# First stage of a fused four-layer kernel: x loaded a second time, already turned, and block loads shared by two queues

## The chip, the cores and the metric

The kernel runs on one NeuronCore of a Trainium2 chip. The metric is the device time of one execution in microseconds (us), as the median of several runs. Below, PE is TensorE, PEld its weight loads, ACT is ScalarE, DVE is VectorE, POOL is GpSimd and SP is SyncE; SPq and ACTq are the instructions with which SyncE and ScalarE issue transfers.

## What is computed

x has 32 batches of 64 channels of 1024 values (f32). Four layers follow one another, each as x = x + ffn(cond(x)). Only the first one is touched:

```
cond, layer 0: out[b] = agg_w[b] (64x64) @ x[b] + agg_b[b]
ffn, layer 0:  logits = out @ route_w^T (8 experts); best one e, its logit v
               h = out @ A^T (8 experts x 16); keep the 16 of e, times v
               ffn = kept h @ Bw
x = x + ffn                      (called x1 below)
cond, layer 1: grouped convolution of x1 along the 1024 values, 9 taps
```

Layers 1 to 3 are a quantised matmul with a row maximum, a routed LoRA layer, and a two-matrix feed-forward with a latent branch and a layer norm.

## The kernel before, in words

The work is cut into NT = 16 tiles of 128 rows (two batches of 64 channels), each 128 x 1024 values, 512 KB. `build` runs `phase_setup`, then `phase_l0` (the first stage), each a block of its own that ends with a barrier of all engines, and then one block for the other three layers, which begins with the convolved tiles of the first stage and with their column maxima. The changed stage, `phase_l0`, contains layer 0 and the convolution of layer 1, as a pipeline over steps s.

In step s TensorE does, in this order: `ph(s)`, the product of the turned tile s with the 136 columns of A and the router (L587); the first half of the convolution of tile s-4 (L437, L438); `mix(s)`, the mixing of the 64 channels (L596); the second half of that convolution; the turning of tile s+1, eight transposes into two PSUM banks (L607); `po(s-1)`, the product with Bw (L614); and the turning of the gated 128 x 128 block of tile s (L619). ScalarE does the copy of ph into h_in (L503), the shifted copies Xs of tile s-3 (L451, L452), for which it waits until all eight block loads of that tile have landed, the two copies of the turned tile s+1 from PSUM into xT (L515), and the copy of the turned gated block, whT (L520). mix(s+1) waits for whT(s) and for h_in(s+1). VectorE finds the best expert (L537 to L552), adds ctx to the convolution result into y1T (L527), takes the column maximum (L559) and adds po to the tile in place, which makes x1 (L566).

SyncE issues all transfers of the stage, tile after tile: it waits for x1 of tile t, stores it to a scratch tensor (L488), waits until the store has landed, loads x of tile t+4 into the slot that came free (L491), and then issues eight block loads of 64 KB each (L446, in `load_windows`) that read the stored tile back as X, the 1024 values cut into eight blocks spread over the partitions:

```
view = dram.rearrange("t (n c) (p k) -> t p c n k", n=2 * GROUPS, p=KC)
for p in range(KC):
    sp.dma_start(dst[p * GI:(p + 1) * GI, :, :], view[t, p]).then_inc(sem, 16)
```

Each block load writes 16 partitions in runs of 512 bytes. The x tiles sit in four slots, X and Xs in three. In `phase_setup` SyncE loads the first four tiles of x (L253); the buffer y1T, 16 slots of one tile, holds weights in its slots 0 to 13 during setup and is filled with the convolved tiles 0 to 15 later. `load_windows` is also called in the block of the later layers (L740); there SyncE issues in each round the store of y2T (L696), in eight rounds a load of 512 KB (L749), the store of x2 (L734, `scratch_x<-l_x`), and waits for that store before the block loads. `eps` is one f32 per partition, used as the bias of a square root in the last layer (L1562); the larger SBUF buffers but for y1T and l2_base are allocated behind it.

Of the kernel before, what the change touches and what calls it, by code (L numbers as in the profile page):

```python
# [11 lines left out]
P = 128  # L12
# [167 lines left out]
def phase_setup(nc, K, A, SC):  # L180


    with ExitStack() as ctx:
# [42 lines left out]
        def _(sp):  # L226
# [25 lines left out]
            for t in range(4):  # L252
                sp.dma_start(K["x"][:, t, :], A["x"][t]).then_inc(K["x_loaded"][t], 16)  # L253
            sp.wait_ge(bias3_out, 1)
# [187 lines left out]
def load_windows(sp, dram, t, dst, sem):  # L442

    view = dram.rearrange("t (n c) (p k) -> t p c n k", n=2 * GROUPS, p=KC)
    for p in range(KC):
        sp.dma_start(dst[p * GI:(p + 1) * GI, :, :], view[t, p]).then_inc(sem, 16)  # L446
# [8 lines left out]
def phase_l0(nc, K, A, SC):  # L455
# [3 lines left out]
    with ExitStack() as ctx:  # L459
        s_ = Scope(nc, ctx)  # L460
        wa, wb, x, X, Xs = K["l0_wa"], K["l0_wb"], K["x"], K["X"], K["Xs"]
        xT = s_.sb("xT", [P, KC, P])
# [7 lines left out]
        pt = s_.banks("pt", 2)  # L470
# [5 lines left out]
        (xT_mm, xT_made, h_mm, hp_made, m_mm, route, wh_made, wh_turned, whT_made, o_mm, x1_made, Xs_made, conv_done,  # L476
         y_made, topped) = s_.sems(
            "xT_mm xT_made h_mm hp_made m_mm route_step wh_made wh_turned whT_made o_mm x1_made Xs_made conv_done "
# [5 lines left out]
        @block.sync  # L484
        def _(sp):
            for t in range(NT):
                sp.wait_ge(x1_made, 2 * (t + 1))
                sp.dma_start(SC["x1"][t], x[:, t % 4, :]).then_inc(x1_stored[t % 4], 16)  # L488
                sp.wait_ge(x1_stored[t % 4], 16 * (t // 4 + 1))
                if t + 4 < NT:  # L490
                    sp.dma_start(x[:, t % 4, :], A["x"][t + 4]).then_inc(K["x_loaded"][t % 4], 16)  # L491
                if t >= 3:
                    sp.wait_ge(conv_done, 2 * (t - 2))
                load_windows(sp, SC["x1"], t, X[t % 3], X_loaded[t % 3])

        @block.scalar
        def _(act):
            for s in range(-1, NT + LAG - 1):
                if 0 <= s < NT:
                    act.wait_ge(h_mm, s + 1)  # L500
                    if s >= 1:
                        act.wait_ge(m_mm, s)
                    act.copy(hp[:], ph[:, 0:P + E0]).then_inc(hp_made, 1)  # L503
                t = s - 3
                if 0 <= t < NT:
                    act.wait_ge(X_loaded[t % 3], 16 * KC * (t // 3 + 1))
                    if t >= 3:
                        act.wait_ge(conv_done, 2 * (t - 2))
                    shift_windows(act, Xs[t % 3], X[t % 3], Xs_made)
                if s + 1 < NT:  # L510
                    for i in range(2):
                        act.wait_ge(xT_mm, 2 * (s + 1) + i + 1)
                        if s >= 0:
                            act.wait_ge(h_mm, s + 1)
                        act.copy(xT[:, 4 * i:4 * i + 4, :], pt[i][:].rearrange("k (p o) -> k p o", p=4)).then_inc(xT_made, 1)  # L515
                if 0 <= s < NT:
                    act.wait_ge(wh_turned, s + 1)
                    if s >= 1:
                        act.wait_ge(o_mm, 2 * s)
                    act.copy(whT[:], pm[:, 2 * P:3 * P]).then_inc(whT_made, 1)  # L520

        @block.vector
        def _(dve):
# [6 lines left out]
            for s in range(NT + LAG):  # L530
# [30 lines left out]
                if 0 <= s - 1 < NT:  # L561
                    slot = x[:, (s - 1) % 4, :]
                    for i in range(2):
                        dve.wait_ge(o_mm, 2 * (s - 1) + i + 1)
                        half = slice(i * HALF, (i + 1) * HALF)
                        dve.tensor_tensor(slot[:, half], po[i][:], slot[:, half], ALU.add).then_inc(x1_made, 1)  # L566
# [3 lines left out]
        def _(pe):  # L570
# [10 lines left out]
            for s in range(-1, NT + LAG):  # L581
                if 0 <= s < NT:
                    pe.wait_ge(xT_made, 2 * (s + 1))
                    if s >= 1:
                        pe.wait_ge(hp_made, s)
                    for k in range(KC):
                        last = pe.matmul(ph[:, 0:P + E0], xT[:, k, :], wa[:, k, :], start=k == 0, stop=k == KC - 1)  # L587
# [11 lines left out]
                if s + 1 < NT:  # L599
                    t = s + 1  # L600
                    pe.wait_ge(K["x_loaded"][t % 4], 16 * (t // 4 + 1))
                    for i in range(2):
                        if t >= 1:
                            pe.wait_ge(xT_made, 2 * (t - 1) + i + 1)
                        for j in range(4):
                            k = 4 * i + j
                            last = pe.transpose(pt[i][:, j * P:(j + 1) * P], x[:, t % 4, k * P:(k + 1) * P], K["ident"][:])  # L607
                        last.then_inc(xT_mm, 1)
# [63 lines left out]
def phase_l1(nc, K, A, SC, s_, buf, ahead):  # L672
# [55 lines left out]
    def sync(sp):  # L728
# [7 lines left out]
        def windows_in(t):  # L736
# [3 lines left out]
            load_windows(sp, SC["x2"], t, X[t % 3], X_loaded[t % 3])  # L740
# [673 lines left out]
def phase_l3(nc, K, A, SC, out, s_, buf):  # L1414
# [122 lines left out]
    def scalar(act):  # L1537
# [15 lines left out]
        def norm(half):  # L1553

            for T in range(HT * half, HT * (half + 1)):
# [6 lines left out]
                act.activation(root[:, T:T + 1], ssq[:, T:T + 1], ACT.Sqrt, bias=eps[:], scale=1.0 / D).then_inc(rooted, 1)  # L1562
# [237 lines left out]
def build(nc, A, out):  # L1800
# [8 lines left out]
    with ExitStack() as ctx:  # L1809
# [10 lines left out]
        K["x_loaded"] = s.slot_sems("x_loaded", 4)  # L1820
# [3 lines left out]
        K["eps"] = s.sb("eps", [P, 1])  # L1824
# [65 lines left out]
def lay_out(i):  # L1890
# [16 lines left out]
    a["x"] = c(feat(i["x"])).reshape(NT, P, D)  # L1907
    cut = {"cT": np.asarray(i["cond_128"]).T}
# [58 lines left out]
```

## Time and profile before

| | |
|---|---|
| median of 3 runs | 1857.82 us (1857.61 to 1861.25) |
| the profiled execution's own time | 1855.62 us |
| its span | 1853.8 us |
| mean granted TensorE clock | 0.973 |
| TensorE busy | 1741.4 us (94%) |
| bytes moved by DMA | 205.80 MB |

The profiled execution stands 2.2 us below the median. A busy time is a sum over the instructions of an engine; idle time of an engine costs something only where the others wait for it. In the timelines each row gives start, duration, engine, line and what is written from what; a bracket at the end tells how long the engine had been idle and who released it. In a timeline of TensorE an f32 product stands as two matmuls. In this text T(t) is the moment at which the store of x1 of tile t has landed, and mix(s) stands for the start of that matmul.

### The profile page before, as it was taken

What the parts mean: (1) busy time and instruction counts of PE and PEld (TensorE: products, weight loads), DVE (VectorE), ACT (ScalarE), POOL (GpSimd) and SP (SyncE); (2) the same over time, 40 slices, a digit from 0 to 9 for tenths busy, and PEclk for the clock granted to TensorE, in tenths of its full rate; (3) what the DMA queues carried; (4) which work ended last, traced back from release to release, by engine and by line L of the source; (5) the groups of instructions that cost most, each with busy time, mean ns of one, the idle gap of its engine ahead of it and who ended that gap; (6) DMA issues with size and microseconds to landing.
All of it is one profiled execution on the core that took longest, in us unless ns stands there. A gap on an engine that the chain in (4) does not pass through costs nothing.

```text
span 1853.8 us, 22240 instructions
## 1 busy us (share of the span) xinstructions
PE 1741.4 (94%) x8396; PEld 1412.5 (76%) x8396; DVE 824.0 (44%) x1453; ACT 459.5 (25%) x694; POOL 340.2 (18%) x186
## 2 busy tenths in 40 slices
PE   7899847999799999999999999999999999999997
PEld 3578736878678888888668888888777888888876
DVE  4256578985524433443323333333272333333326
ACT  2344323433311111111132222221123222222212
POOL 1000011234223333333311111111201111111110
PEclk9899978999899999999999999999999999999999
DMA  8377323566533223332751111111292111111114
GB/s 308 95 193 191 114 71 124 180 194 220 207 97 117 93 95 106 117 93 83 200 178 56 46 46 45 45 45 46 98 333 69 46 46 46 45 45 45 46 57 159
DMA packets 126803, 205.80 MB, mean 111 GB/s; under 512 B 14436, under 2 KB 82092, under 8 KB 126124
## 3 DMA queue, kind: packets, MB, share of 16 engines
q1 hardware_dynamic: 109716, 158.41, 26.8%
q0 software_dynamic: 11264, 27.27, 4.6%
q10 hardware_dynamic: 5760, 19.27, 3.2%
q8 instruction: 42, 0.69, 0.2%
q14 instruction: 21, 0.17, 0.0%
HBM read 143.01 MB, written 61.89 MB: 111 GB/s over the span
## 4 chain that ended last, share of the span: by engine, by line
PE 72%; DVE 6%; DMA 5%; SPq 1%; issue 1%; ACT 1%; POOL 0%; DVEq 0%; ACTq 0%
PE pd L1410 24%; PE pu L1410 24%; PE l_po L1410 18%; PE pf L1410 2%; DMA scratch_x<-l_x 2%; PE l_py L1384 1%; PE l_pr L1368 1%; DVE row_peak L836 1%; DMA l_base_lo<-scratch_y_lo 1%; SPq L446 1%; DMA l_B_raw<-in_l_B 1%; DMA scratch_y_lo<-y_out_lo 1%; PE l_pc L1334 1%; DVE y1T L861 1%; ACT row_mag L791 1%
## 5 line engine op out<-in xcount | busy, mean ns | idle before, releaser
L1410 PE MATMUL pu<-l_base_hi,up_hi 128*128 128x512 f32 x640 | 253.4, 396 | 0.0
L1410 PE MATMUL pu<-l_base_lo,up_hi 128*128 128x512 f32 x640 | 252.9, 395 | 0.0
L1410 PE MATMUL pu<-l_base_hi,up_lo 128*128 128x512 f32 x640 | 252.9, 395 | 0.0
L1410 PE MATMUL pd<-down_hi,hid_hi 128*128 128x512 f32 x640 | 250.1, 391 | 2.9 <-issue 2.9
L1410 PE MATMUL pd<-down_hi,hid_lo 128*128 128x512 f32 x640 | 249.5, 390 | 0.0
L1410 PE MATMUL pd<-down_lo,hid_hi 128*128 128x512 f32 x640 | 249.5, 390 | 0.0
L1533 POOL TENSOR_TENSOR down_lo<-raw,down_hi 128x1024 fp32r<-128x1024 f32 x40 | 100.4, 2511 | 716.4 <-ACT down_hi L1546 716.4
L1698 DVE TENSOR_TENSOR hid_lo<-hidden,hid_hi 128x512 fp32r<-128x512 f32 x64 | 44.8, 701 | 406.4 <-ACT hid_hi L1607 406.4
L1638 DVE TENSOR_TENSOR acc<-pd,acc 128x512 f32<-128x512 f32 x224 | 144.0, 686 | 56.4 <-PE pd L1410 53.5
L1601 ACT ACTIVATE hidden<-pu 128x512 f32<-128x512 f32 x64 | 38.3, 598 | 474.5 <-PE pu L1410 474.5
L1410 PEld LDWEIGHTS pd<-down_hi,hid_hi 128*128 128x128 f32 x640 | 120.1, 188 | 29.7 <-issue 3.7
L1410 PEld LDWEIGHTS pu<-l_base_hi,up_lo 128*128 128x128 f32 x640 | 120.1, 188 | 29.4
L1410 PEld LDWEIGHTS pu<-l_base_hi,up_hi 128*128 128x128 f32 x640 | 120.1, 188 | 28.9
L1410 PEld LDWEIGHTS pu<-l_base_lo,up_hi 128*128 128x128 f32 x640 | 120.1, 188 | 28.7
L1410 PEld LDWEIGHTS pd<-down_hi,hid_lo 128*128 128x128 f32 x640 | 120.1, 188 | 26.0
L1410 PEld LDWEIGHTS pd<-down_lo,hid_hi 128*128 128x128 f32 x640 | 120.1, 188 | 25.9
L1410 PE MATMUL pf<-cbT,z_hi 128*128 128x512 f32 x256 | 108.1, 422 | 18.3 <-DVE z_lo L876 18.1
L1410 PE MATMUL l_po<-l_B_hi,crT_hi 128*128 128x512 f32 x256 | 103.2, 403 | 3.5 <-DVE crT_lo L1255 3.5
L1264 DVE TENSOR_TENSOR l_y<-l_py,l_bias 128x512 f32<-128x512 f32 x32 | 22.1, 692 | 187.0 <-issue 97.0
L1410 PE MATMUL pf<-cbT,z_lo 128*128 128x512 f32 x256 | 104.7, 409 | 0.0
L1410 PE MATMUL l_po<-l_base_hi,l_y2s_hi 128*128 128x512 f32 x256 | 103.9, 406 | 0.0
L1410 PE MATMUL l_po<-l_base_hi,l_y2s_lo 128*128 128x512 f32 x256 | 101.2, 395 | 0.0
(244 smaller groups left out, 2850.9 us busy)
## 6 DMA issues: line engine op xcount, KB each, us to landing
X<-scratch_x SPq DMA_DIRECT2D x256, 64.0 KB, 2.7
l_x<-scratch_x SPq DMA_DIRECT2D x32, 512.0 KB, 4.8
raw<-in_up SPq DMA_DIRECT2D x32, 512.0 KB, 3.5
raw<-in_down SPq DMA_DIRECT2D x32, 512.0 KB, 4.2
x_in<-in_x SPq DMA_DIRECT2D x16, 512.0 KB, 4.2
scratch_x<-x_in SPq DMA_DIRECT2D x16, 512.0 KB, 3.3
scratch_x<-l_x SPq DMA_DIRECT2D x16, 512.0 KB, 5.1
scratch_y2T<-y2T SPq DMA_DIRECT2D x16, 512.0 KB, 3.0
```

The costliest lines, as they stand in the source:

```text
L446: sp.dma_start(dst[p * GI:(p + 1) * GI, :, :], view[t, p]).then_inc(sem, 16)
L791: act.activation(mag[:, 0:n, p, :], y[:, t0:t0 + n, 4 * i + p, :], ACT.Abs, scale=keep[:, 4 * i + p:4 * i + p + 1]).then_inc(mag_made, 1)
L836: dve.tensor_reduce(peak[:, i, 0:n, :].unsqueeze(3), mag[:, 0:n, :, :].rearrange("k t p j -> k t j p"), AX.X, ALU.max).then_inc(peaked, 1)
L861: dve.tensor_tensor(y[:, t0 + j, :, :], y[:, t0 + j, :, :], pb[:, j * P:(j + 1) * P].unsqueeze(1).to_broadcast([P, KC, P]), ALU.mult).then ...
L1264: dve.tensor_tensor(y3[:, h * HALF:(h + 1) * HALF].rearrange("p (c k) -> p c k", c=4), py[h][:].rearrange("p (c k) -> p c k", c=4), bias3[ ...
L1334: last = pe.transpose(pc[h][:, j * P:(j + 1) * P], cr[:, k * P:(k + 1) * P], K["ident"][:])
L1368: last = pe.matmul(pr[0][0:R2 + E2, 0:P], war[:, k, :], y2[:, k * P:(k + 1) * P], start=k == 0, stop=k == KC - 1)
L1410: mm = pe.matmul(out, lhs[a], rhs[b], start=first and n == 0, stop=last and n == len(pairs) - 1)
L1533: pool.tensor_tensor(dn[u][i][1][:], raw[i][:], dn[u][i][0][:].bitcast(F32), ALU.subtract).then_inc(dn_lo, 1)
L1601: act.activation(act_f[:, k % 2, :], pu[q], ACT.Relu).then_inc(relu, 1)
L1638: last = dve.tensor_tensor(part, bank, part, ALU.add)
L1698: dve.tensor_tensor(hid[u][1][:, i, cols], pu[q] if lat else act_f[:, k % 2, :], hid[u][0][:, i, cols].bitcast(F32), ALU.subtract).then_in ...
```

## The change

- x is also laid out turned on the host (`xT`: tile, value within a block, block, row), 16 more tiles of 512 KB in. The slots for it are the slots 14, 15, 12 and 13 of y1T. Tiles 0 and 1 are loaded in setup between the x tiles, tiles 2 and 3 at the start of the stage, and tile t+4 by SyncE in its iteration t, ahead of the store of x1(t), once ph(t) is done.
- TensorE's eight transposes of a tile and ScalarE's two copies are gone. ph(s) waits for the load of its turned tile.
- SyncE issues five of the eight block loads of a tile in the first stage, ScalarE the other three, in step s for tile s-2, behind its copies Xs of tile s-3 and ahead of whT(s). For that it waits for the landed store of tile s-2. In the later layers SyncE issues all eight, as before.
- VectorE waits for the load of the x tile, to which it adds.
- eps has 16 values per partition instead of one; the first is used.

```diff
@@ phase_setup, SyncE
             for t in range(4):
                 sp.dma_start(K["x"][:, t, :], A["x"][t]).then_inc(K["x_loaded"][t], 16)
+                if t < 2:
+                    sp.dma_start(K["xT"][t], A["xT"][t]).then_inc(K["xT_loaded"][t], 16)
@@
-def load_windows(sp, dram, t, dst, sem):
+def load_windows(eng, dram, t, dst, sem, phases):
...
-    for p in range(KC):
-        sp.dma_start(dst[p * GI:(p + 1) * GI, :, :], view[t, p]).then_inc(sem, 16)
+    for p in phases:
+        eng.dma_start(dst[p * GI:(p + 1) * GI, :, :], view[t, p]).then_inc(sem, 16)
@@ phase_l0, SyncE
+            for t in range(2, 4):
+                sp.dma_start(K["xT"][t], A["xT"][t]).then_inc(K["xT_loaded"][t], 16)
             for t in range(NT):
+                if t + 4 < NT:
+                    sp.wait_ge(h_mm, t + 1)
+                    sp.dma_start(K["xT"][t % 4], A["xT"][t + 4]).then_inc(K["xT_loaded"][t % 4], 16)
                 sp.wait_ge(x1_made, 2 * (t + 1))
...
-                load_windows(sp, SC["x1"], t, X[t % 3], X_loaded[t % 3])
+                load_windows(sp, SC["x1"], t, X[t % 3], X_loaded[t % 3], range(5))
@@ phase_l0, ScalarE
-                if s + 1 < NT:
-                    for i in range(2):
-                        act.wait_ge(xT_mm, 2 * (s + 1) + i + 1)
-                        if s >= 0:
-                            act.wait_ge(h_mm, s + 1)
-                        act.copy(xT[:, 4 * i:4 * i + 4, :], pt[i][:].rearrange("k (p o) -> k p o", p=4)).then_inc(xT_made, 1)
-                if 0 <= s < NT:
+                t = s - 2
+                if 0 <= t < NT:
+                    act.wait_ge(x1_stored[t % 4], 16 * (t // 4 + 1))
+                    if t >= 3:
+                        act.wait_ge(conv_done, 2 * (t - 2))
+                    load_windows(act, SC["x1"], t, X[t % 3], X_loaded[t % 3], range(5, KC))
+                if s < NT:
                     act.wait_ge(wh_turned, s + 1)
@@ phase_l0, VectorE
                     slot = x[:, (s - 1) % 4, :]
+                    dve.wait_ge(K["x_loaded"][(s - 1) % 4], 16 * ((s - 1) // 4 + 1))
@@ phase_l0, TensorE
-                    pe.wait_ge(xT_made, 2 * (s + 1))
+                    pe.wait_ge(K["xT_loaded"][s % 4], 16 * (s // 4 + 1))
...
-                        last = pe.matmul(ph[:, 0:P + E0], xT[:, k, :], wa[:, k, :], start=k == 0, stop=k == KC - 1)
+                        last = pe.matmul(ph[:, 0:P + E0], K["xT"][s % 4][:, k, :], wa[:, k, :], start=k == 0, stop=k == KC - 1)
...
-                if s + 1 < NT:
-                    t = s + 1
-                    pe.wait_ge(K["x_loaded"][t % 4], 16 * (t // 4 + 1))
-                    for i in range(2):
-                        if t >= 1:
-                            pe.wait_ge(xT_made, 2 * (t - 1) + i + 1)
-                        for j in range(4):
-                            k = 4 * i + j
-                            last = pe.transpose(pt[i][:, j * P:(j + 1) * P], x[:, t % 4, k * P:(k + 1) * P], K["ident"][:])
-                        last.then_inc(xT_mm, 1)
@@ build
+        K["xT"] = [K["y1T"][:, t, :, :] for t in (14, 15, 12, 13)]
-        K["eps"] = s.sb("eps", [P, 1])
+        K["eps"] = s.sb("eps", [P, 16])
@@ lay_out
+    a["xT"] = c(a["x"].reshape(NT, P, KC, P).transpose(0, 3, 2, 1))
```

## Rows read from the trace of the kernel before

**Rows 1.** The page: busy us of each engine, share of the span, instructions.

```profile
PE 1741.4 (94%) x8396; PEld 1412.5 (76%) x8396; DVE 824.0 (44%) x1453; ACT 459.5 (25%) x694; POOL 340.2 (18%) x186
```

**Rows 2.** Stretches: busy us of PE, PEld, DVE, ACT, POOL; clock, DMA share, GB/s.

```profile
75.00:84.00 9.00, 7.63 (x32) 6.94 (x33) 0.74 (x3) 1.44 (x3) 0.00 (x0) 0.50 0.01 3
...
104.90:108.00 3.10, 3.08 (x14) 3.08 (x15) 0.00 (x0) 0.14 (x1) 0.00 (x0) 0.52 1.06 205
108.00:202.00 94.00, 94.00 (x714) 82.91 (x713) 57.16 (x121) 42.05 (x69) 0.00 (x0) 1.00 0.67 186
```

**Rows 3.** Timeline of TensorE, one step in the middle (convolutions left out).

```profile
148.25 2.02 PE L587 MATMUL ph<-l_wa,xT 128*128 128x136 f32 x16
...
151.89 0.40 PE L596 MATMUL pmix<-h_in,mats 128*128 128x136 f32 x2
...
153.91 1.04 PE L607 MATMUL pt<-ident,x_in 128*128 128x128 f32 x8
154.78 1.88 PE L614 MATMUL po<-l_wb,whT 128*128 128x512 f32 x4
...
156.61 1.56 PE L587 MATMUL ph<-l_wa,xT 128*128 128x136 f32 x12
```

**Rows 4.** Timeline of SyncE's transfers, first tiles; last row: what L491 waited for.

```profile
91.49 0.33 SPq L488 DMA_DIRECT2D scratch_x<-x_in  x1
94.12 0.33 SPq L491 DMA_DIRECT2D x_in<-in_x  x1
94.50 3.74 SPq L446 DMA_DIRECT2D X<-scratch_x  x8
98.28 0.43 SPq L488 DMA_DIRECT2D scratch_x<-x_in  x1
102.61 0.35 SPq L491 DMA_DIRECT2D x_in<-in_x  x1
...
110.89 0.35 SPq L491 DMA_DIRECT2D x_in<-in_x  x1
...
SPq L491 <- DMA scratch_x<-x_in: 36.6, 12, 3.9
```

**Rows 5.** Timeline of TensorE, start and end of the stage.

```profile
75.33 1.94 PE L607 MATMUL pt<-ident,x_in 128*128 128x128 f32 x8 [4.68 <-PEq L104]
77.95 3.99 PE L587 MATMUL ph<-l_wa,xT 128*128 128x136 f32 x16 [0.68 <-ACT xT L515]
...
104.92 3.55 PE L587 MATMUL ph<-l_wa,xT 128*128 128x136 f32 x16 [3.24 <-ACT xT L515]
...
202.05 0.40 PE L596 MATMUL pmix<-h_in,mats 128*128 128x136 f32 x2
```

**Rows 6.** ScalarE: the first wait for block loads; the copies of the turned tile.

```profile
101.67 1.04 ACT L451 COPY Xs<-X 64x1016 f32<-64x1016 f32 x1 [3.25 <-DMA X<-scratch_x]
...
L515 ACT COPY xT<-pt 128x512 f32<-128x512 f32 x32 | 17.3, 589 | 17.7 <-PE pt L607 17.7
```

**Rows 7.** The chain of waits in the second layer: start us, us, what.

```profile
402.81 0.36 SPq L696
403.22 0.43 SPq L749
403.69 5.91 DMA scratch_x<-l_x
...
414.64 7.20 DMA scratch_x<-l_x
...
426.50 6.63 DMA scratch_x<-l_x
```

**Rows 8.** ScalarE's own transfers in the third layer: ns of one issue.

```profile
L1195 ACTq DMA_DIRECT2D l_y<-scratch_y2T x14: 344/344/372, 510.1 to 851.7; - x14
```

**Rows 9.** VectorE groups: one on buffers allocated before eps, one behind it.

```profile
L410 DVE TENSOR_REDUCE w_scb<-y1T 128x1 f32<-128x1024 f32 x8 | 9.4, 1214 | 10.0 <-DMA y1T<-in_L_ffn_weight 9.9
...
L1245 DVE TENSOR_TENSOR l_B_lo<-l_B_raw,l_B_hi 128x1024 fp32r<-128x1024 f32 x8 | 9.2, 1221 | 9.6 <-ACT l_B_hi L1189 9.6
```

More of the change, by code:

```diff
@@ L469, in phase_l0 @@
         key, gain = small[:, 8:16], small[:, 16:24]
-        pt = s_.banks("pt", 2)
         (ph,) = s_.banks("ph", 1)
@@ L475, in phase_l0 @@
         x1_stored, X_loaded = s_.slot_sems("x1_stored", 4), s_.slot_sems("X_loaded", 3)
-        (xT_mm, xT_made, h_mm, hp_made, m_mm, route, wh_made, wh_turned, whT_made, o_mm, x1_made, Xs_made, conv_done,
+        (h_mm, hp_made, m_mm, route, wh_made, wh_turned, whT_made, o_mm, x1_made, Xs_made, conv_done,
          y_made, topped) = s_.sems(
-            "xT_mm xT_made h_mm hp_made m_mm route_step wh_made wh_turned whT_made o_mm x1_made Xs_made conv_done "
+            "h_mm hp_made m_mm route_step wh_made wh_turned whT_made o_mm x1_made Xs_made conv_done "
             "y1_made y1_topped")
@@ L493, in _ @@
                     sp.wait_ge(conv_done, 2 * (t - 2))
-                load_windows(sp, SC["x1"], t, X[t % 3], X_loaded[t % 3])
+                load_windows(sp, SC["x1"], t, X[t % 3], X_loaded[t % 3], range(5))
         @block.scalar
         def _(act):
-            for s in range(-1, NT + LAG - 1):
-                if 0 <= s < NT:
+            for s in range(NT + LAG - 1):
+                if s < NT:
                     act.wait_ge(h_mm, s + 1)
@@ L509, in _ @@
                     shift_windows(act, Xs[t % 3], X[t % 3], Xs_made)
-                if s + 1 < NT:
-                    for i in range(2):
-                        act.wait_ge(xT_mm, 2 * (s + 1) + i + 1)
-                        if s >= 0:
-                            act.wait_ge(h_mm, s + 1)
-                        act.copy(xT[:, 4 * i:4 * i + 4, :], pt[i][:].rearrange("k (p o) -> k p o", p=4)).then_inc(xT_made, 1)
-                if 0 <= s < NT:
+                t = s - 2
[4 more added lines that the diff above has]
+                    load_windows(act, SC["x1"], t, X[t % 3], X_loaded[t % 3], range(5, KC))
+                if s < NT:
                     act.wait_ge(wh_turned, s + 1)
@@ L579, in conv @@
                 conv_windows(pe, pv[b][:], K["taps"][0], X[t % 3], Xs[t % 3], b).then_inc(conv_done, 1)
-            for s in range(-1, NT + LAG):
-                if 0 <= s < NT:
-                    pe.wait_ge(xT_made, 2 * (s + 1))
+            for s in range(NT + LAG):
+                if s < NT:
+                    pe.wait_ge(K["xT_loaded"][s % 4], 16 * (s // 4 + 1))
                     if s >= 1:
@@ L739, in windows_in @@
                 sp.wait_ge(conv_done, 2 * (t - 2))
-            load_windows(sp, SC["x2"], t, X[t % 3], X_loaded[t % 3])
+            load_windows(sp, SC["x2"], t, X[t % 3], X_loaded[t % 3], range(KC))
         for s in range(NT):
@@ L1561, in norm @@
                 act.wait_ge(ssq_made, T + 1)
-                act.activation(root[:, T:T + 1], ssq[:, T:T + 1], ACT.Sqrt, bias=eps[:], scale=1.0 / D).then_inc(rooted, 1)
+                act.activation(root[:, T:T + 1], ssq[:, T:T + 1], ACT.Sqrt, bias=eps[:, 0:1], scale=1.0 / D).then_inc(rooted, 1)
                 if 0 < T % HT < HT - 1:
@@ L1819, in build @@
         K["x3b_loaded"], K["y3_loaded"] = s.slot_sems("x3b_loaded"), s.slot_sems("y3_loaded")
-        K["x_loaded"] = s.slot_sems("x_loaded", 4)
+        K["x_loaded"], K["xT_loaded"] = s.slot_sems("x_loaded", 4), s.slot_sems("xT_loaded", 4)
+        K["xT"] = [K["y1T"][:, t, :, :] for t in (14, 15, 12, 13)]
         K["g_stored"] = s.slot_sems("g_stored")
```

1 line of the change is left out of this document (removed).

## The prediction

> **What bounds the kernel now.** The page first: TensorE is busy in 94% of the span [rows 1], so idle time elsewhere says little by itself. The changed stage lies between two barriers, about 75 to 232 us; what is saved in it moves the rest forward as a block, and nothing behind the second barrier can hide it. So only the stage has to be read, and I cut it into stretches [rows 2]. From 108 to 202 TensorE is busy without a gap at full clock while the DMA engines are busy 0.67 of the time. The timeline of one step shows why [rows 3]: ph starts at 148.25 and the next ph at 156.61, a period of 8.36 us, in which the eight transposes take 0.87 (153.91 to 154.78). In the middle of the stage TensorE ends last.
>
> The second reading is SyncE's queue [rows 4], because it runs nearly as long. At the start, where TensorE's steps hold no convolution and are short, SyncE sets the pace: load of x at 94.12, again at 102.61 and 110.89, cycles of 8.49 and 8.28, mean 8.4. Such a cycle is one load issue, eight block loads (3.74, so 0.47 each), one store issue, and 4.3 (98.28 to 102.61) until that store has landed. A store with nothing ahead of it lands in 2.6 (91.49 to 94.12). Over the stage the wait before L491 is 36.6 us in 12 [rows 4], 3.05 each; with the store's 0.34 and the rest of the cycle (0.38 + 3.74 + 0.04) it needs 7.6 without any queueing behind its own backlog and 8.4 with it. So SyncE stands only 0 to 0.8 behind TensorE's 8.36, and whoever shortens TensorE's step meets SyncE at once.
>
> **The change, part by part.**
>
> *Transposes gone.* 0.87 per step where TensorE binds: 8.36 - 0.87 = 7.49 is TensorE's new period. Over the 11 steps from mix(4) to mix(15) that is at most 9.6 us.
>
> *Copies gone.* ScalarE loses 32 x 0.589 = 17.3 us [rows 6]. Twice these copies were on the path. At the start, ph(0) waited for transposes and copies: 75.33 to 77.95, 2.6 us [rows 5]; this goes, the turned tile 0 is loaded in setup. At step 4 ph stood 3.24 us behind them, because ScalarE was held at 101.67 by the first block loads, and then ran 104.92 to 108.47 at a clock of 0.52 [rows 2, 5, 6], the lower level of 1.2 GHz, after the idle stretch. What is late next there is the shifted copy itself, which still waits for the block loads.
>
> *Loads of xT.* 16 issues. Tiles 0 and 1 queue in setup, where SyncE has nothing to issue for some 20 us before the barrier; tiles 2 and 3 are issued while SyncE would wait for its first store at 91.49. Priced at nothing; if that cover failed, a queue of two transfers would delay setup by 1.2 each, 2.4. From tile 4 on each stands in SyncE's queue ahead of the store: 0.47 for the issue, and the store queues behind its data. The nearest rows are in the second layer [rows 7]: two transfers of this size (L696, L749) stand between the block loads and the store there, and the store takes 5.91, 7.20 and 6.63 to land, mean 6.6, against 4.3 right behind the block loads: 1.15 for each transfer, at most 1.45. Bounds: 0, if the data fit into the third of the time in which the DMA engines are idle [rows 2], and 1.45. I take 1.2, as rows 7 have the same queue and size.
>
> *Three block loads to ScalarE.* SyncE issues 3 x 0.47 = 1.41 less per cycle. ScalarE pays 3 x 0.344 [rows 8] plus gaps, 1.2, behind a wait for the landed store. Queued behind them are whT(s) and h_in(s+1), for both of which mix(s+1) waits. So mix(t+3) starts no sooner than T(t) + 1.2 + 0.3 + 0.3, about T(t) + 2.0. In the steady step mix starts 3.6 after ph (148.25, 151.89), so this wait has that room and costs nothing unless SyncE is late.
> The row says that SyncE's issue time is on the cycle: its store at 98.28 goes out as soon as the last block load is issued (98.24). The Trainium skill (DMA: Bandwidth & Descriptors, section Issuing engines are not separate DMA queues) speaks against this part: transfers issued by several engines run on the same 16 DMA engines, and only the issue time is saved, usually small beside the transfer. By that rule read strictly, with the data as the bound, the 1.41 would not come off; what this would give is the third rival.
>
> *SyncE's new cycle c.* 8.4 + 0.47 + 1.2 - 1.41 = 8.66 from the cycles in which it sets the pace. The same from the cycle without backlog, 7.6, is 7.9. I take 8.5, nearer the first, since SyncE would now always set the pace.
>
> *eps and the wait on x.* Where buffers begin changes for nearly everything. A reduction that reads y1T (before eps) takes 1214 ns, a subtraction with all operands behind it 1221 [rows 9]: the place makes no visible difference. Bounds -1 to +1 us, taken 0. VectorE's wait is for a load issued some three steps earlier: 0.
>
> **The sum.** ph(0) starts 2.6 earlier, so the first store would go out at 91.49 - 2.6 = 88.9; I add 0.6: until 84 the granted clock is 0.50 [rows 2], a ph at it takes 3.99 [rows 5] against 2.02 [rows 3], and with the transposes gone TensorE does less there, so the rise may come later; 0.6 is a third of that difference. With 2.6 to land, T(0) = 92.1. SyncE then needs twelve cycles to T(12), the last without a turned tile (1.6 less): 92.1 + 12 x 8.5 - 1.6 = 192.5. mix(15) follows at +2.0: 194.5, against 202.05 [rows 5], so 7.5 saved. At the end of the stage the chain is store, block loads, shifted copy, convolution; SyncE issues three block loads less before the last store and three less behind it, 1.41 twice at most, of which I take 1.6, since x1 of the last tile is not ready much earlier. Together 9.1. Against the profiled execution's own 1855.62 this gives 1846.5; the median lies 2.2 above it, so **1848.7**.
>
> **The rivals.**
>
> *TensorE stays the bound* (c at most 7.5). For it: the DMA engines are busy only 0.67 of the time [rows 2], and the lower estimate of c, 7.9, is not far off. Against it: the landings in rows 7. mix(4) would come at T(1) + 2.0 to 2.3 = 101.9, mix(15) 11 x 7.49 later at 184.3, 17.8 earlier, with the end 19.4: 1838.4.
>
> *The queue gives half back* (c about 9.2). xT's data cost their full 1.45 and half of the 1.41 returns as queueing. T(12) = 92.1 + 110.4 - 1.6 = 200.9, mix(15) 202.9, 0.8 late, the end 1.6 early: 1857.0, no change that can be told.
>
> *Slower: transfers bind.* Before, a cycle moved three tiles' worth (x, block loads, store); now four, on the same DMA engines, with a share of 1.06 at only 205 GB/s in 104.9 to 108 [rows 2], where block loads and a store meet. If the data are the bound, the 1.41 saved in issuing come back whole: c = 8.5 + 1.41 = 9.9, T(12) = 209.3, mix(15) 211.3, 9.2 late, less 1.6: 7.6 slower, 1865.4. It decides from c = 9.26 on (92.1 + 12c - 1.6 + 2.0 = 203.65). Against it: 4 tiles in 9.9 us would be only 212 GB/s. This is also where the Trainium skill leads (same page and section as above); the trace bears it out in part, since in the middle the share is far from 1.
>
> *The change does less than it says*: that xT makes ph wait. It is issued three steps ahead, so only if the whole queue is late, which is the rival before. 0.03, time near before.
>
> **How the numbers follow.** About 0.2% (3.7 us) is what a measurement of this kernel can tell from no change. c from 8.0 to 8.9 (15.1 to 4.3 saved): 0.48. c under 8.0 or TensorE the bound: 0.20. c from 8.9 to 9.6 (4.3 saved to 4.1 lost) 0.17, with the change that does less 0.03. c above 9.6: 0.12. Faster is the first two and a little of the third, 0.70; within 0.2% 0.18; slower 0.12. The range reaches from TensorE as the bound, 1838, to c = 9.3 and a lost microsecond in setup, 1859; it leaves out about 0.05 below and 0.14 above.
>
> **What would show it.** L607 and L515 gone; first ph near 75.3; 8.4 MB more moved. The cycle of L491 in the middle at 8.5 with the store landing in 5 to 5.5, and small gaps on TensorE before mix, released by ScalarE. If instead TensorE is gapless with period 7.5, the first rival holds; if the share of the DMA engines is near 1 and the store takes 7, the third. ScalarE's three issues far over 0.4 each would be a wait that I have not priced. Matmuls of the later layers longer or shorter than before would prove me wrong on eps.

## The result, and the profile after

The changed kernel takes 1867.34 us (median of 10 runs, 1864.68 to 1870.30) against 1855.93 (median of 10, 1849.22 to 1861.25) for the kernel before on the same chip: ratio 1.0063, 95% interval 1.0050 to 1.0075. It is slower, by some 11 us. The forecast was 1848.7 with a range up to 1859. The profiled execution took 1870.0, its span is 1868.2 and the mean granted clock 0.974, as before.

The page first, busy time of each engine as in [rows 1]:

```profile
PE 1725.1 (92%) x8268; PEld 1400.4 (75%) x8268; DVE 824.2 (44%) x1453; ACT 441.0 (24%) x662; POOL 340.1 (18%) x186
```

TensorE has 128 instructions and 16.3 us less, ScalarE 32 instructions and 18.5 us less, and the time went up: work was taken away and waiting came in. Where it came in is told by the first instruction behind the second barrier, VectorE's column maximum; here it is in the timeline of VectorE, before and then after.

```profile
232.23 0.38 DVE L890 TENSOR_REDUCE col_max<-col_top 128x8 f32<-128x128 f32 x1 [1.25 <-PEq L104]
```

```profile
250.35 0.38 DVE L886 TENSOR_REDUCE col_max<-col_top 128x8 f32<-128x128 f32 x1 [1.22 <-PEq L104]
```

The changed stage ends 18.1 us later. What follows takes 1868.2 - 250.35 = 1617.9 against 1853.8 - 232.23 = 1621.6, so 3.7 us less. These are two separate effects.

Stretches of the kernel after, with the columns of [rows 2]:

```profile
75.00:84.00 9.00, 6.08 (x24) 5.48 (x25) 1.49 (x6) 0.54 (x2) 0.00 (x0) 0.50 0.49 176
...
108.00:202.00 94.00, 75.88 (x500) 63.27 (x499) 48.24 (x101) 22.60 (x36) 0.00 (x0) 0.96 0.81 204
```

In the middle of the stage TensorE was busy for 94.00 of 94 us before; now it is busy for 75.88. Over the whole stage, by the same view from 75 us to its end, it works 6.7 us less (137.28 against 143.99) and idles 24.8 us more (38.0 against 13.2): together the 18.1. The DMA engines' share in the middle rose from 0.67 to 0.81.

SyncE's queue, in the timeline of its transfers, is the view that explains it (compare [rows 4]):

```profile
91.22 0.33 SPq L493 DMA_DIRECT2D scratch_x<-x_in  x1
93.84 0.33 SPq L496 DMA_DIRECT2D x_in<-in_x  x1
...
97.06 0.43 SPq L493 DMA_DIRECT2D scratch_x<-x_in  x1
...
145.29 0.33 SPq L496 DMA_DIRECT2D x_in<-in_x  x1
145.67 2.33 SPq L448 DMA_DIRECT2D X<-scratch_x  x5
148.04 0.43 SPq L491 DMA_DIRECT2D y1T<-in_xT  x1
148.52 0.43 SPq L493 DMA_DIRECT2D scratch_x<-x_in  x1
155.41 0.33 SPq L496 DMA_DIRECT2D x_in<-in_x  x1
...
209.65 0.43 SPq L493 DMA_DIRECT2D scratch_x<-x_in  x1
215.35 2.20 SPq L448 DMA_DIRECT2D X<-scratch_x  x5
```

The first store still lands in 2.62 (91.22 to 93.84). In the middle the issue of x load, five block loads, turned load and store takes 3.66 us (145.29 to 148.95), less than before, but the store takes 6.89 to land (148.52 to 155.41), and nothing else happens in SyncE meanwhile. The cycle is 155.41 - 145.29 = 10.12. The waits of SyncE in this stage say the same:

```profile
SPq L496 <- DMA scratch_x<-x_in: 74.7, 12, 7.6
...
SPq L493 <- DVE x_in L572: 11.1, 1, 11.1
```

The wait for the landed store before the load of x was 36.6 in 12 [rows 4] and is 74.7 in 12. The last line matters as much: only once, for the first tile, does the store wait for x1. From then on SyncE is held by its own chain alone: store landed, x load, block loads, turned load, store.

How the data run inside one such cycle, in stretches with the same columns:

```profile
145.30:147.30 2.00, 2.00 (x15) 2.00 (x16) 0.00 (x0) 0.44 (x2) 0.00 (x0) 0.81 0.24 67
147.30:148.50 1.20, 1.20 (x8) 1.20 (x7) 0.69 (x2) 0.00 (x0) 0.00 (x0) 0.50 0.96 367
148.50:150.50 2.00, 2.00 (x14) 2.00 (x13) 1.39 (x6) 0.00 (x0) 0.00 (x0) 0.64 1.25 187
150.50:152.50 2.00, 2.00 (x9) 0.99 (x8) 1.54 (x2) 0.00 (x0) 0.00 (x0) 1.00 1.16 194
152.50:155.40 2.90, 2.13 (x19) 1.96 (x17) 1.56 (x3) 2.08 (x2) 0.00 (x0) 1.00 0.66 263
```

What moves there is told by the size of the packets, in the view of the DMA queues for the third of these stretches (the runs of a block load are 512 bytes; these 792 packets hold 470 bytes on average):

```profile
DMA packets 792, 0.37 MB, mean 187 GB/s; under 512 B 91, under 2 KB 788, under 8 KB 792
```

First almost nothing moves (67 GB/s, the transfers are only being issued), then mostly the x load, at 367 GB/s. Then for 2 us nearly all packets are those of block loads, at 187 GB/s and a share of the DMA engines of 1.25, and for 2 us more the last of them (233 of 303 packets) together with the turned load, at 194. Only then the rest of the turned load and the store follow. The turned load lands at 154.1, 6.1 us after its issue, and the store 1.3 us behind it. The mean of 0.81 hides that the engines are full just while the store waits in line.

On the other engines: ph(0) at last starts at once, but it and the next ph run at the lower clock (1.2 GHz, granted 0.50), and TensorE has no gap before mix(4). TensorE's timeline:

```profile
75.80 3.96 PE L593 MATMUL ph<-l_wa,y1T 128*128 128x136 f32 x16 [4.68 <-PEq L104]
...
82.97 3.83 PE L593 MATMUL ph<-l_wa,y1T 128*128 128x136 f32 x16
...
105.42 0.50 PE L602 MATMUL pmix<-h_in,mats 128*128 128x136 f32 x2
...
206.67 0.46 PE L439 MATMUL pv<-taps,X 128*128 128x128 f32 x2 [2.60 <-issue]
...
218.29 0.40 PE L602 MATMUL pmix<-h_in,mats 128*128 128x136 f32 x2
```

The same ph(1) took 2.12 in the kernel before, from its timeline of TensorE:

```profile
85.16 2.12 PE L587 MATMUL ph<-l_wa,xT 128*128 128x136 f32 x16
```

In the kernel after, the gaps stand before the convolution (206.67), which waits for block loads and shifted copies; before mix there are only two behind the first steps, 0.23 at mix(6) and 0.73 at mix(12). ScalarE's timeline in the first of these steps:

```profile
103.50 1.32 ACTq L448 DMA_DIRECT2D X<-scratch_x  x3
104.92 0.27 ACT L525 COPY whT<-pmix 128x128 f32<-128x128 f32 x1 [1.62 <-issue]
```

Its three issues take 1.32, so 0.44 each (0.344 was taken). mix(4) starts at 105.42, 1.92 after the landing at 103.50; 2.0 was taken.

### The profile page after: what moved, and what is told of

Read it like the earlier page. It is cut to its first block, busy times and chain, and to the rows that moved or that the text cites. A ratio compares the mean times of both kernels' runs of the same rounds, so it can differ in the third digit from the quotient of the medians.

```text
span 1868.2 us, 21952 instructions
## 1 busy us (share of the span) xinstructions
PE 1725.1 (92%) x8268; PEld 1400.4 (75%) x8268; DVE 824.2 (44%) x1453; ACT 441.0 (24%) x662; POOL 340.1 (18%) x186
## 4 chain that ended last, share of the span: by engine, by line
PE 71%; DVE 7%; DMA 5%; SPq 1%; issue 1%; ACT 1%; POOL 0%; DVEq 0%; ACTq 0%
PE pd L1406 24%; PE pu L1406 23%; PE l_po L1406 18%; PE pf L1406 2%; DMA scratch_x<-l_x 2%; PE l_py L1380 1%; PE l_pr L1364 1%; DVE row_peak L832 1%; DMA l_base_lo<-scratch_y_lo 1%; SPq L448 1%; DMA l_B_raw<-in_l_B 1%; DVE y1T L857 1%; DMA scratch_y_lo<-y_out_lo 1%; PE l_pc L1330 1%; DVE z_lo L872 1%
## 5 line engine op out<-in xcount | busy, mean ns | idle before, releaser
L1406 PE MATMUL l_po<-l_B_hi,crT_lo 128*128 128x512 f32 x256 | 101.3, 396 | 0.0
```

The source lines that it names most:

```text
L1406: mm = pe.matmul(out, lhs[a], rhs[b], start=first and n == 0, stop=last and n == len(pairs) - 1)
```

## The experiments

The theory from the result: the store of x1 stands in SyncE's queue behind the turned load, inside a loop that is serial (landed store, x load, block loads, turned load, store); and what the three block loads save in issue comes back as a later landing. Rivals: ScalarE's issues are what costs; the partitions of the block loads are written in a bad order; the data volume binds, wherever the load stands. To compare them I use one number of each trace, the **mean cycle**: the 11 cycles between the start of the second store and that of the thirteenth. It is (191.46 - 98.28) / 11 = 8.47 before and (209.65 - 97.06) / 11 = 10.24 after.

The last column covers the stores inside these 11 cycles. In e5, e6 and e8 it is the time until the first block load goes out, since no load of x marks the landing. How far traces of the same stage lie apart is told by two pairs that differ in the size of eps alone: 8.47 and 8.56 (before, e7), 10.24 and 10.07 (after, e9).

| kernel | median us | ratio to before, 95% | mean cycle | store lands in |
|---|---|---|---|---|
| before | 1855.93 | | 8.47 | 3.0 to 4.3 |
| after | 1867.34 | 1.0063 [1.0050, 1.0075] | 10.24 | 6.4 to 8.0 |
| e1 after, all eight on SyncE | 1870.57 | 1.0084 [1.0054, 1.0114] | 10.27 | 5.3 to 5.7 |
| e2 before, with the split | 1859.56 | 1.0026 [1.0013, 1.0039] | 8.79 | 4.1 to 6.6 |
| e3 turned load behind the store | 1847.01 | 0.9965 [0.9944, 0.9986] | 8.69 | 5.3 to 7.2 |
| e4 no turned loads 4 to 15 | 1849.24 | 0.9967 [0.9949, 0.9984] | 8.33 | 4.7 to 6.0 |
| e12 e4, all eight on SyncE | 1846.43 | 0.9960 [0.9945, 0.9974] | 8.40 | 3.3 to 4.6 |
| e11 turned loads on GpSimd | 1858.11 | 1.0015 [1.0001, 1.0028] | 9.35 | 4.8 to 8.3 |
| e10 e1, other order of blocks | 1867.76 | 1.0058 [1.0040, 1.0076] | 10.30 | 5.2 to 5.5 |
| e5 both loads behind the store, all on SyncE | 1844.96 | 0.9952 [0.9937, 0.9967] | 8.18 | 3.3 to 6.7 |
| e6 the same with the split | 1835.01 | 0.9887 [0.9866, 0.9908] | 7.34 | 3.5 to 6.0 |
| e8 before, x load behind the store | 1863.94 | 1.0041 [1.0021, 1.0061] | 9.04 | 2.9 to 3.5 |
| e7 before, eps of 64 bytes | 1850.45 | 0.9968 [0.9954, 0.9982] | 8.56 | 3.1 to 4.4 |
| e9 after, eps of 4 bytes | 1871.03 | 1.0086 [1.0070, 1.0102] | 10.07 | 6.3 to 8.3 |

### What the split is worth

**e1: the changed kernel with all eight block loads on SyncE.**

```diff
-                load_windows(sp, SC["x1"], t, X[t % 3], X_loaded[t % 3], range(5))
+                load_windows(sp, SC["x1"], t, X[t % 3], X_loaded[t % 3], range(KC))
@@ ScalarE
-                    load_windows(act, SC["x1"], t, X[t % 3], X_loaded[t % 3], range(5, KC))
```

> The changed kernel, but SyncE issues all eight block loads again. Theory A (position in the queue: the store of x1 stands behind the load of the turned tile): the cycle of SyncE stays long, 10.2 plus at most the three issues, 1.4; 1867 to 1882 us, store landing in 5.5 to 7 us. Theory B (data: four tiles' worth per cycle keep the DMA engines busy, issue time is hidden): cycle 10.2, 1867. Theory C (the split itself costs, since ScalarE's block loads run beside SyncE's and ScalarE's copies wait behind them): the cycle falls below 9.5 and the time below 1862.

Measured 1870.57, mean cycle 10.27 against 10.24 with the split. SyncE's timeline in one cycle:

```profile
142.00 0.33 SPq L496 DMA_DIRECT2D x_in<-in_x  x1
142.38 3.74 SPq L448 DMA_DIRECT2D X<-scratch_x  x8
146.17 0.43 SPq L491 DMA_DIRECT2D y1T<-in_xT  x1
146.64 0.43 SPq L493 DMA_DIRECT2D scratch_x<-x_in  x1
152.02 0.33 SPq L496 DMA_DIRECT2D x_in<-in_x  x1
```

The block loads take 3.74 to issue, 1.41 more than the 2.33 for five, and the store lands in 5.38 instead of 6.89, 1.51 less. The cycle is the same. The turned load ahead of the store lands at 150.8 here, 4.6 us after its issue, and the store 1.2 us behind it, where that was 1.3 with the split: with or without it the store lands when the data ahead of it are through. Theory C is out; A and B both allowed this result and are told apart by e3. The intervals of e1 and of the changed kernel overlap, so no gain or loss of the split can be told in the time.

**e2: the kernel before with the split alone.** ScalarE issues block loads 5 to 7 behind its shifted copies; the rest is as before.

```diff
-                load_windows(sp, SC["x1"], t, X[t % 3], X_loaded[t % 3])
+                load_windows(sp, SC["x1"], t, X[t % 3], X_loaded[t % 3], range(5))
@@ ScalarE, behind shift_windows
+                    load_windows(act, SC["x1"], t, X[t % 3], X_loaded[t % 3], range(5, KC))
```

> The kernel before, with three of eight block loads issued by ScalarE and nothing else changed; no turned load. Theory A: SyncE gains 1.4 us per cycle where it sets the pace, which is at the start and the end only, TensorE's 8.36 stays in the middle; 1850 to 1855. Theory B: the same, 1853 to 1856, since the data of a cycle are as before. Theory C: slower than before, 1858 to 1865, with gaps on TensorE before mix.

Measured 1859.56, a little slower than before, as theory C had it and A and B had not. The mean cycle did not fall; it is 8.79 (8.47 before), and the store lands in 5.1 to 5.8 in the middle where it took 3.1 to 4.2. So the split alone saved nothing here either. But this kernel has a cost of its own, which the changed kernel doesn't have. Timeline of ScalarE, last row TensorE:

```profile
133.60 1.33 ACTq L446 DMA_DIRECT2D X<-scratch_x  x3
135.02 1.07 ACT L521 COPY xT<-pt 128x512 f32<-128x512 f32 x2 [1.14 <-issue]
...
136.15 2.12 PE L593 MATMUL ph<-l_wa,xT 128*128 128x136 f32 x16 [0.70 <-ACT xT L521]
```

The copies of the turned tile still exist here. They stand behind ScalarE's wait for the landed store (133.59) and its three issues, and TensorE waits for them before ph: 5.5 us in 6 between 100 and 210. Its gaps are before ph and not before mix, so theory C names the right engine and another step. e2 is therefore not a clean measure of the split; e1 and e12 are. In the traced execution TensorE moreover begins the stage 3.8 us late (79.13 against 75.33), though nothing ahead of the stage differs; the stage itself takes only 1.4 us longer than before.

**e12: no turned loads from tile 4 on, all eight on SyncE**, the partner of e4 below.

> The changed kernel with the loads of the turned tiles 4 to 15 left out and all eight block loads on SyncE; ph of these steps reads the turned tiles 0 to 3 again, so layer 0 of twelve tiles is computed on other data. If the cycle is a chain of data, x, block loads, store, in which the split saves nothing, it equals the one with the split (8.3 to 8.5) and the time lies within 3 us of 1849, with the landing near 4.3 instead of 5.6. If the split did save its 1.4 us there, the cycle here is 9.7 and the time 1863.

```profile
SPq L493 <- DMA scratch_x<-x_in: 39.4, 12, 3.9
```

Mean cycle 8.40, with the split (e4) 8.33; 1846.43 against 1849.24, intervals that overlap. This pair too differs in nothing but the split, and its 1.41 us per cycle come back whole again.

### What the turned load costs, and whether its place or its bytes cost it

**e4: the turned loads of tiles 4 to 15 left out.**

```diff
                 if t + 4 < NT:
-                    sp.wait_ge(h_mm, t + 1)
-                    sp.dma_start(K["xT"][t % 4], A["xT"][t + 4]).then_inc(K["xT_loaded"][t % 4], 16)
```

> The changed kernel with the loads of the turned tiles 4 to 15 left out; ph of these steps reads the turned tiles 0 to 3 again, so layer 0 of twelve tiles is computed on other data and the time is that of the stage without these transfers. Theory A and theory B both: the store lands in 4 to 4.5, cycle 7.6 to 8.0 and the time 1838 to 1846; this is the price of the twelve turned loads, 1.9 to 2.5 us each. Theory C: the cycle stays above 9 and the time above 1856.

Mean cycle 8.33 against 10.24: a turned load ahead of the store costs 1.91 with the split, and 10.27 - 8.40 = 1.87 without it (e1 and e12). Time, cycle and landing (4.7 to 6.0) all came out above what was expected, the landing by about the 1.4 that the split was still taken to save.

**e3: the turned load right behind the store.** All transfers stay.

```diff
                 sp.dma_start(SC["x1"][t], x[:, t % 4, :]).then_inc(x1_stored[t % 4], 16)
+                if t + 4 < NT:
+                    sp.wait_ge(h_mm, t + 1)
+                    sp.dma_start(K["xT"][t % 4], A["xT"][t + 4]).then_inc(K["xT_loaded"][t % 4], 16)
                 sp.wait_ge(x1_stored[t % 4], 16 * (t // 4 + 1))
```

> The changed kernel, but the load of the turned tile is issued right behind the store of x1 instead of ahead of it; same transfers, same number. Theory A: the store lands in 3.5 to 4.5 us again instead of 6.8, the turned load fills the time in which SyncE waits; cycle 7.8 to 8.3, 1840 to 1848. Theory B: the data bind in any order, cycle 9.7 to 10.2, 1861 to 1867. Theory C: as B.

1847.01, some 20 us below the changed kernel, from one transfer moved by one place. Stretch from 108 to 202 of this kernel:

```profile
108.00:202.00 94.00, 84.53 (x602) 71.69 (x603) 56.62 (x121) 28.59 (x46) 0.00 (x0) 1.00 0.88 234
```

The DMA engines now move 234 GB/s where they moved 204. The bytes do not bind as such; their order does. Of the 1.91 us per cycle 1.55 are gone (10.24 to 8.69). The time is as theory A had it, the landing is not: 5.3 to 7.2 instead of 3.5 to 4.5. It is near that of e4, which has no turned load but has the split, too.

**e11: the turned loads issued by GpSimd**, which has nothing else to do in this stage, as soon as ph(t) is done.

```diff
+        @block.gpsimd
+        def _(pool):
+            for t in range(NT - 4):
+                pool.wait_ge(h_mm, t + 1)
+                pool.dma_start(K["xT"][t % 4], A["xT"][t + 4]).then_inc(later_loaded[t % 4], 16)
```

> The changed kernel with the turned tiles 4 to 15 issued by GpSimd, as soon as ph of the slot's old tile is done; SyncE's queue holds x, block loads and stores only. Theory A (the place in SyncE's queue right ahead of the store is what costs): the cycle falls from 10.2 to 8.3 to 9.0, as with the load right behind the store, 1845 to 1853 us. Theory B (any load in flight beside the store costs the same wherever it is issued): 9.7 to 10.3, 1862 to 1869.

Neither value came: 1858.11, and the cycles alternate. Timelines of GpSimd, then of SyncE:

```profile
133.78 0.53 POOL L503 DMA_DIRECT2D y1T<-in_xT  x1 [11.97 <-PE ph L600]
141.26 0.53 POOL L503 DMA_DIRECT2D y1T<-in_xT  x1 [6.96 <-PE ph L600]
```

```profile
134.31 0.43 SPq L491 DMA_DIRECT2D scratch_x<-x_in  x1
142.32 0.35 SPq L494 DMA_DIRECT2D x_in<-in_x  x1
...
145.36 0.43 SPq L491 DMA_DIRECT2D scratch_x<-x_in  x1
151.02 0.35 SPq L494 DMA_DIRECT2D x_in<-in_x  x1
```

The store at 134.31, with a turned load issued half a microsecond earlier on another queue (133.78), lands in 8.01; the store at 145.36, with the turned load 4.1 us earlier (141.26), in 5.66. Another queue doesn't take the load out of the store's way; a time at which the store isn't under way does. That the distance alone decides is read from these rows, not tested by itself.

**e10: e1 with the block loads in the order 0, 4, 1, 5, 2, 6, 3, 7**, so that neighbours in the queue write distant partitions.

> The changed kernel with all eight block loads on SyncE, issued in the order 0, 4, 1, 5, 2, 6, 3, 7 of their partition groups instead of 0 to 7. Block p writes partitions 16p to 16p+15. If the data of the block loads are slow because neighbouring loads in flight write to the same part of SBUF (the Trainium skill, SBUF — State Buffer, section Door 1: The DMA port swizzle, gives partitions 0 to 63 one half of the ports and 64 to 127 the other), alternating halves shortens the cycle from 10.2 to 8.5 to 9.5 and the time from 1870.6 to 1850 to 1863. If the runs of 512 bytes themselves set the pace on the DMA engines, nothing changes: 1868 to 1873.

Mean cycle 10.30 against 10.27, 1867.76 against 1870.57 with intervals that overlap. The two halves of the ports of which the Trainium skill speaks (SBUF — State Buffer, section Door 1: The DMA port swizzle) did not show: in this pair the order made no difference.

### How far the order carries, and what it needs

**e5 and e6: turned load and x load both behind the store**, the x load for tile t+3 instead of t+4, since the slot of tile t is only then being stored. e5 with all eight block loads on SyncE, e6 with the split.

```diff
                 sp.dma_start(SC["x1"][t], x[:, t % 4, :]).then_inc(x1_stored[t % 4], 16)
+                if t + 4 < NT:
+                    sp.wait_ge(h_mm, t + 1)
+                    sp.dma_start(K["xT"][t % 4], A["xT"][t + 4]).then_inc(K["xT_loaded"][t % 4], 16)
+                if t >= 1 and t + 3 < NT:
+                    sp.dma_start(x[:, (t + 3) % 4, :], A["x"][t + 3]).then_inc(K["x_loaded"][(t + 3) % 4], 16)
                 sp.wait_ge(x1_stored[t % 4], 16 * (t // 4 + 1))
-                if t + 4 < NT:
-                    sp.dma_start(x[:, t % 4, :], A["x"][t + 4]).then_inc(K["x_loaded"][t % 4], 16)
```

> The changed kernel with SyncE issuing all eight block loads, and with both big loads, the turned tile t+4 and x of tile t+3, issued right behind the store of x1(t), so that the block loads come first once it has landed. Theory A' (what counts is which data lie in the loop from one landed store to the next; here block loads and store alone): eight issues 3.75, store issue 0.43, landing 3.2 to 4.2: cycle 7.5 to 8.3, near TensorE's own 7.5; 1838 to 1845 us. Theory B (all data of a cycle bind, 2.1 MB at the 206 GB/s seen in the changed kernel): cycle 10, 1865.

> As the run before, with three of eight block loads issued by ScalarE as in the change. If the issue time saved returns whole as a later landing, as the pair with all block loads on SyncE showed for the change (cycle 10.2 with and without the split, landing 6.9 against 5.35), the time is within 3 us of the run before, with a landing longer by 1 to 1.5 us. If the split helps once the loads are out of the way, 3 to 8 us faster.

e6 takes 1835.01, the fastest of all kernels here, 21 us below the kernel before and 32 below the changed one. Stretch and SyncE's timeline of e6:

```profile
108.00:190.00 82.00, 82.00 (x603) 70.81 (x602) 56.55 (x122) 28.79 (x46) 0.00 (x0) 1.00 0.98 272
```

```profile
146.37 0.34 SPq L490 DMA_DIRECT2D scratch_x<-x_in  x1
146.75 0.45 SPq L493 DMA_DIRECT2D y1T<-in_xT  x1
...
153.86 0.34 SPq L490 DMA_DIRECT2D scratch_x<-x_in  x1
...
SPq L490 <- DVE x_in L572: 22.9, 8, 14.8
```

TensorE is busy without a gap for 82 us, and the period is 7.49 (146.37 to 153.86), the 8.36 less 0.87 that the prediction had worked out for TensorE as the bound. SyncE waits for x1 again, 8 times. Against e3, where only the turned load stands behind the store, the cycle falls from 8.69 to 7.34 and the time by 12 us. e5, without the split, takes 1844.96, so **here the split is worth 10 us** (the intervals are far apart), though it was worth nothing in two other pairs. Seven of e5's cycles are 7.0 to 7.7, one is 8.7 and three are about 10; the mean is 8.18. These three make 7.0 of the 9.2 us between the two traces. SyncE in the first of them, and below it the waits of e5 for the landed store:

```profile
108.20 0.43 SPq L490 DMA_DIRECT2D scratch_x<-x_in  x1
...
114.90 3.91 SPq L448 DMA_DIRECT2D X<-scratch_x  x8
...
SPq L448 <- DMA scratch_x<-x_in: 37.7, 16, 4.9
```

The block loads are late because the store itself lands late, 6.7 us after its issue (6.3 and 4.6 in the other two, 3.3 to 3.8 otherwise); the convolution that frees the slot of X is done 5 us earlier (its last matmul starts at 109.31). So a store with the two large loads behind it can still be late; in e6 it was once (6.0). Why was not tried. The other eight cycles gain 2.1 us together, 0.3 each for 1.41 of issue time; in five of its eleven cycles e6 stands at TensorE's 7.49 and can't gain more.

**e8: the kernel before with the x load behind the store**, the reordering without the change.

```diff
                 sp.dma_start(SC["x1"][t], x[:, t % 4, :]).then_inc(x1_stored[t % 4], 16)
+                if t >= 1 and t + 3 < NT:
+                    sp.dma_start(x[:, (t + 3) % 4, :], A["x"][t + 3]).then_inc(K["x_loaded"][(t + 3) % 4], 16)
```

> The kernel before with the load of x of tile t+3 issued right behind the store of x1(t), in place of the load of t+4 behind the landed store. Theory A': the loop at the start falls from 8.4 to 7.5 or so, TensorE's 8.36 stays in the middle, the first block loads land 0.5 to 1.5 us earlier: 1851 to 1856 us. Theory B: no change, 1855 to 1857.

A miss: 1863.94, slower than before. The store does land in 2.9, but the mean cycle is 9.04. The view of L607, the transposes, tells how long TensorE and its weight loads sat idle ahead of them in this kernel, and until what (us, times):

```profile
  DMA x_in<-in_x: 16.7, 14
...
  ACT xT L515: 37.0, 18
```

The kernel before has no such wait for a load of x, and the wait of ScalarE for these transposes (the last line) was 17.7 there [rows 6]. TensorE turns tile s+1 within step s and so needs x sooner than VectorE does; a load only three tiles ahead comes too late for it. With x turned on the host only VectorE needs the x tile, and late. So the order of e6 does its work only together with the host's turning.

### The constant's size

**e7: the kernel before with eps of 64 bytes, nothing else; e9: the changed kernel with eps of 4 bytes.**

```diff
-        K["eps"] = s.sb("eps", [P, 1])
+        K["eps"] = s.sb("eps", [P, 16])
```

> The kernel before with the constant of 64 bytes and nothing else changed. My prediction priced it at 0, bounds -1 to +1 us: 1855 to 1857, ratio 0.9995 to 1.0005. The rival, that the place of the buffers behind it changes matmuls or transfers, asks for over 2 us either way and a changed mean duration of the matmuls into pu or pd, or another landing time of the block loads.

> The changed kernel with the constant back at 4 bytes. Alone, the 64 bytes made the kernel before 5.2 us faster, and the matmuls into pu went from 396 to 392 ns. If that gain is a thing of the last layer and adds up, this run takes 1871 to 1874 us, 4 to 7 more than the changed kernel's 1867, and pu is back at 396 ns. If it came from the transfers of the first stage, the cycle of SyncE here is longer than 10.2 us. If the first result was scatter, 1866 to 1868.

e7 is faster than before, 0.9968 [0.9954, 0.9982], some 5 us. The groups of matmuls in the last layer show where. The kernel before:

```profile
L1410 PE MATMUL pu<-l_base_hi,up_hi 128*128 128x512 f32 x640 | 253.4, 396 | 0.0
...
L1410 PE MATMUL pd<-down_hi,hid_hi 128*128 128x512 f32 x640 | 250.1, 391 | 2.9 <-issue 2.9
```

and e7:

```profile
L1410 PE MATMUL pu<-l_base_hi,up_hi 128*128 128x512 f32 x640 | 251.0, 392 | 0.0
```

A matmul of the first product of that layer (pu, three groups of 640) takes 392 ns instead of 395 or 396; those of the second product (pd) stay at 390 or 391. All ten traces with 64 bytes read 392 in this group, all four with 4 bytes 396. From the first to the last pu it is 864.9 us in e7 and 869.4 before. e9 reads 396 ns again and 868.7 (864.2 in the changed kernel, with 64 bytes). So the constant's size gives 4.5 us in that layer in both kernels. From the second barrier to the end the ten traces with 64 bytes take 1613.8 to 1621.5 us, mean 1618.0, the four with 4 bytes 1619.7 to 1625.1, mean 1621.7. Single traces scatter there by several us, but the means differ by 3.7, as before and after do. The medians agree with that (1871.03 against 1867.34), though the intervals of the two ratios touch.

## Why the prediction was wrong

Direction and size were both missed. The end of the stage was forecast at 232.23 - 9.1 = 223.1 and came at 250.35, 27.2 late (rounded); the later layers gave 3.7 back; together 23.5, which is the profiled execution's 1870.0 less the 1846.5 of the sum. The 27.2 by the prediction's own steps:

- **Start, T(0) = 92.1.** 93.84, 1.7 late. The turned tiles did not delay setup (ph(0) at 75.80, with nothing but the barrier ahead of it). But ph(1) too ran at the lower clock (3.83 instead of 2.12: the whole difference, where a third was taken). That the missing transposes are the reason is not shown: in e1, e3, e5 and e12, without them as well, ph(1) took 2.02 or 2.03, in e4, e6, e9 and e11 3.83. So it differs from trace to trace, and T(0) with it, from 90.3 (e5) to 94.1 (e4) in the variants of the changed kernel.
- **The turned load, 0.47 + 1.2 = 1.67 per cycle.** 1.9 in both pairs. Right in kind and nearly in size: less the 0.47 of the issue it is 1.4 for the data, the upper bound (1.45) of the rows of the second layer.
- **The split, -1.41 per cycle. This is the step that failed.** Measured: 10.24 - 10.27 = -0.03 and 8.33 - 8.40 = -0.07 (e2's +0.32 holds ScalarE's copies, too). The prediction saw in [rows 4] that the store is issued as soon as the last block load is, and took the issue time to be on the cycle. It is on the cycle of issues; but the store lands when the data ahead of it have gone through, and these are behind by then. The store was issued 1.4 us sooner in the cycle and took 1.5 us longer to land.
- **The cycle.** 8.4 + 1.9 + 0 = 10.3 against 10.24 measured; 8.5 was taken. The base of 8.4 held: it is 8.40 in e12, which has neither split nor turned loads. Of the 1.74 missed, the split makes 1.4; the rest is the turned load, sized 0.2 too low, and the step from 8.66 down to 8.5. Over the twelve cycles to T(12) = 215.35 this is 121.5 instead of 100.4, so 21.1 of the 27.2.
- **mix(t+3) at T(t) + 2.0.** 1.92 at mix(4), 2.94 at mix(15) (218.29), 0.9 late. ScalarE's wait was costed rightly at nothing on the path.
- **The tail, 1.6 less.** From mix(15) to the end 32.1 instead of 30.2: 1.9 more, so 3.5 off the forecast. The last landings take 3.7 to 5.4 where they took 2.6 to 3.2, and 2.9 in e1; but e1's tail is 32.5, so the split saved 0.4 there at the most. The 1.9 beyond before are not explained; e9, the same stage, has a tail of 29.7, so a single trace can't tell a difference of this size.
- **eps, 0 between -1 and +1.** 4.5 us less in the last layer, outside its bounds. The rows chosen [rows 9] were of VectorE; the resource that reacted was TensorE. The page of before already had the hint, pu at 396 ns beside pd at 391 in the same shape, and I did not use it.

**The rivals.** TensorE as the bound was not what happened, though e6 shows its period of 7.49 to be real. The third rival, with 0.12, is what happened in its numbers: issue saved comes back whole, c = 9.9, 1865.4, against 10.24 and 1867.34. Its reason, that the bytes of a cycle bind, holds only in that order: e3 and e6 move the same bytes in cycles of 8.69 and 7.34. The Trainium skill's rule beside it (DMA: Bandwidth & Descriptors, section Issuing engines are not separate DMA queues), that a second issuing engine saves only issue time, agrees: nothing was saved in two pairs (after and e1, e4 and e12), and 0.84 per cycle in the third (e5 and e6), less than the 1.41 moved.

The argument that made that rival unlikely was the mean share of 0.67 [rows 2] and the 212 GB/s that it implied. Both are means. The stretches inside a cycle of the changed kernel show a share above 1 at only 187 and 194 GB/s while block loads are under way. The one row of before that showed such a stretch, 1.06 at 205 GB/s, was quoted in the prediction and outweighed by the mean. In a serial loop it is the stretch that the awaited transfer stands behind that counts.

## What to carry to other kernels

In a loop where one queue waits for a store and then issues loads, ask of each transfer whether it stands ahead of the awaited one; a 512 KB load that nobody needs soon goes right behind the store, not ahead of it (20 us here for one move). Issue time saved by a second queue was worth nothing here while data ahead of the awaited transfer were still moving, and 10 us once the large loads were out of the way, most of it in three late landings that aren't explained; so fix the order first and try the split second. Read the DMA share in stretches of one cycle, not over the stage.

## What the runs showed of the hardware

- Three block loads issued by ScalarE instead of SyncE: the same cycle to 0.1 us in two pairs, with the store landing in 6.9 instead of 5.4.
- The turned load on GpSimd's queue delayed a store on SyncE's queue no less than one ahead of it on the same queue (8.01 to land in e11 and 6.89 in the changed kernel, against 5.5 to 5.7 where they did not meet). Why the meetings alternate from tile to tile stays open.
- The block loads moved 187 GB/s at a share of 1.25, where it was 367 GB/s at a share of 0.96 while mostly the x load moved. The order of their partitions was not the reason (e10). What is wasn't tried.
- 60 more bytes in front of the buffers made 1920 matmuls about 1% shorter and left 1920 others of the same shape alone (e7, e9). Which buffer's place does it wasn't tried.
